# Causal masks of an attention kernel: added to the scores by matmuls with the identity, where GpSimd multiplied behind the exponentials

## The chip, the cores and the metric

The kernel runs on all 8 cores of one Trainium2 chip. The metric is the device time in microseconds of the slowest core. The program is the same on every core; core 2b + h works on batch row b and on the query blocks of parity h. Engines are named as in the profile: PE (TensorE matmul), PEld (its weight loads), DVE (VectorE), ACT (ScalarE), POOL (GpSimd), SP (the engine that issues most DMAs).

## The reference, cut to what matters

One transformer layer: attention, add, layernorm, quantized feed-forward network, add, layernorm.

```python
q = rms_norm((x @ Wq) by heads, q_g)          # 16 heads; only the first 32 of 64 columns are used
kv = x @ Wkv
k = rms_norm((kv @ Wk) by heads, k_g)         # 32 columns a head
v_c = (kv @ Wv) by heads                      # 32 columns a head
scores = jnp.einsum('bhtr,bhsr->bhts', q[..., :32], k) / sqrt(64)
scores = jnp.where(causal, -jnp.inf, scores)  # keys behind the query are masked out
probs = softmax(scores)
out_c = jnp.einsum('bhts,bhsd->bhtd', probs, v_c)
x = layernorm(x + out @ Wo)
# FFN: weights quantized to -1, 0, 1 by their mean; activations to 8 bits by their row's maximum
x = layernorm(x + bitlinear(silu(bitlinear(x, w_gate)) * bitlinear(x, w_up), w_down))
```

Batch 4, 4096 positions, width 1024, inner width 4096.

## The kernel before, in words

**Attention** (`attention()`, L801 on) goes over 4 tiles of 512 queries (`tc`), 4 groups of 4 heads (`gi`) and, for each, over blocks of 128 keys (`sc`). There are 8 key blocks for the first tile, 16, 24 and 32 for the others, thus 4 x (8 + 16 + 24 + 32) = 320 steps. In a step PE makes four score matmuls (L830), one a head, each with 32 rows of the array (`tile_position=(32 * j, 0)`), each into a PSUM bank of its own in `ps_sc`; the four share the array. Keys lie on the partitions of the score, queries along its free axis. ACT takes the exponential in two halves of two heads each (L843) and writes bf16 into one of three buffers `PT`. Two steps later (`LAG = 2`) PE adds the columns up (`den_mms`, L785, weights of ones) and multiplies by the values (`pv_mms`, L796), both with 32 columns of the array a head.

**The mask.** Of each tile's key blocks the last 8 touch the diagonal, which makes 4 x 4 x 8 = 128 diagonal steps; their score matmuls cover only the columns from `stc` on (512, 384, 256 or 128 of them, twice each). Blocks come in pairs, one of the core's own parity (even `sc`) and one of the other (odd `sc`). Of the 128 columns from `stc` on, the even block is triangular, and the odd block is to be kept whole on cores with h = 1 and dropped whole on cores with h = 0. POOL does that behind the exponentials, for the four heads at once: L851 multiplies by the triangle `tri`, L856 by the core's flag `hflag`. `den_mms` of the step waits for that product.

**What is woven in.** `attention()` yields once a step, and twice a step when the FFN has begun (`ffn_on`). At a yield the program puts other work into the queues of the engines in an order that is fixed when the program is built. In the early part, these are the projections of the later queries and keys (L528, L547, L569, L578 on PE) and the stream of FFN weights (`stream_step`): load, sum of absolute values (L366 on DVE, L370 on ACT), quantize (L382, L385 on DVE), store as fp8. When these are over, each yield brings in matmuls of the FFN: `RATE / 2` is added to a credit, and the FFN takes four matmuls of 512 columns at a time from it (L1001 for the up and gate projections, L1124 for the down projection). So a step has 7 FFN matmuls on average. Every engine takes its instructions strictly in this order. In this part the four score matmuls stand one behind the other; in the early part the sums of the step before last (`den_mms`) stand between the first two and the last two. Behind the attention the rest of the FFN runs by itself.

**Others on POOL.** POOL also issues the loads of x (`load_x`, L146), takes the variance to the power -0.5 for the layernorms (L695, L698), and multiplies and rounds in the quantization of the FFN's inner activations (L1073), which DVE (L1076) and a transposing DMA finish ahead of L1124.

Of the kernel before, what the change touches and what calls it, by code (L numbers as in the profile page):

```python
# [7 lines left out]
F32 = mybir.dt.float32  # L8
# [99 lines left out]
def build_nc():  # L108
# [20 lines left out]
    with es:  # L129
# [3 lines left out]
        def pe(fn, after=(), sig=False):  # L133
            return P.op("tensor", fn, after, cT if sig else None)
# [4 lines left out]
        def dve(fn, after=()):  # L139
            return P.op("vector", fn, after, cV)  # L140

        def pool(fn, after=()):
            return P.op("gpsimd", fn, after, cG)
# [4 lines left out]
        def xpose(out, in_, s, after=()):  # L148
# [3 lines left out]
        psb = lambda name, shape, dt: es.enter_context(nc.psum_tensor(name, shape, dt))  # L152


        tri = sb("tri", [128, 128], BF16)
        bd32 = sb("bd32", [128, 128], BF16)
        ones32 = sb("ones32", [128, 32], BF16)
        mhalf = sb("mhalf", [128, 1], F32)
        epsc = sb("epsc", [128, 1], F32)
# [1 line left out]
        hflag = sb("hflag_sb", [128, 1], F32)  # L161
        gq = sb("gq", [128, 1], F32)
        negM = sb("negM", [128, 1], F32)
        wabs = sb("wabs", [128, 48], F32)
        wsum = sb("wsum", [128, 3], F32)
        swb = sb("swb", [128, 3], F32)
        wscl = sb("wscl", [128, 3], F32)
# [39 lines left out]
        wv = rv(16640, 256).bitcast(BF16)  # L207
        onesf = rv(16896, 128)
        grow = rv(17024, 64)
        wq = rv(6144, 4096).bitcast(BF16)  # L210
        xt = [rv(10240 + 2048 * k, 2048).bitcast(BF16) for k in range(2)]
        xqT = [S[:, 1024 * k:1024 * k + 1024].bitcast(BF16) for k in range(2)]
# [36 lines left out]
        t_eps = pool(lambda e: e.memset(epsc[:], 1e-6))  # L249
        pool(lambda e: e.memset(onesf, 1.0))  # L250
        pool(lambda e: e.memset(ones32[:], 1.0))
        t = pool(lambda e: e.memset(tri[:], 1.0))
        pool(lambda e: e.affine_select(tri[:], tri[:], [[1, 128]], ALU.is_ge, 0.0,
                                       base=0, channel_multiplier=-1), [t])
        t = pool(lambda e: e.memset(bd32[:], 1.0))
        for j in range(4):
            t = pool(lambda e, j=j: e.affine_select(
                bd32[:, 32 * j:32 * j + 32], bd32[:, 32 * j:32 * j + 32], [[0, 32]],
# [7 lines left out]

        t = dve(lambda e: e.scalar_tensor_tensor(gq[:], gcol[:, 0:1], 0.125, gcol[:, 1:2],
                                                 ALU.mult, ALU.mult), [t_small])
        t = dve(lambda e: e.tensor_mul(grow[:, 0:32], grow[:, 0:32], grow[:, 32:64]), [t_small])
        t = dve(lambda e: e.tensor_reduce(negM[:], grow[:, 0:32], AX, ALU.max,  # L270
                                          apply_absolute_value=True), [t])
# [164 lines left out]
        def inv_rms(t_sq, inv, banks):  # L436

            b2 = banks.take()
            p2 = banks.bufs[b2]
            for n, (i, tt) in enumerate(t_sq):  # L440
                t2 = pe(lambda e, i=i, n=n, p2=p2: e.matmul(
                    p2, bd32[:], sq[i], start=(n == 0), stop=(n == len(t_sq) - 1)),
                    [tt, banks.free[b2], t_const], n == len(t_sq) - 1)
            for i, tt in t_sq:
                sq_free[i] = t2
            k = n_rs[0] % 2
            n_rs[0] += 1
            t3 = act(lambda e, k=k, p2=p2: e.activation(  # L448
                rsb[k], p2, AF.Ln, bias=epsc[:, 0:1], scale=inv), [t2, t_eps, rs_free[k]])
            banks.give(b2, t3)  # L450
            t4 = act(lambda e, k=k: e.activation(rsb[k], rsb[k], AF.Exp, scale=-0.5), [t3])
            return k, t4
# [360 lines left out]
        def attention():  # L813
# [3 lines left out]
            for tc in range(4):  # L817
                while t_tile[tc] is None:
                    next(proj_it, None)
                for gi in range(4):  # L820
                    smax = 8 * tc + 8
                    for sc in range(smax):
# [3 lines left out]
                        kc = ((2 * (j0 // 4) + sc % 2) * 4 + gi) * 512 + (j0 % 4) * 128  # L826
                        old = pend.pop(0) if len(pend) == LAG else None
                        t_sc = []
                        for j in range(4):
                            t = pe(lambda e, j=j, gi=gi, tc=tc, kc=kc, stc=stc: e.matmul(  # L830
                                ps_sc[:, j * 512 + stc:j * 512 + 512],
                                khat[32 * j:32 * j + 32, kc:kc + 128],
                                qn[32 * j:32 * j + 32, tc * 2048 + gi * 512 + stc:
                                   tc * 2048 + gi * 512 + 512],
                                start=True, stop=True, tile_position=(32 * j, 0)),
                                (sc_free[j // 2] if j % 2 == 0 else [])
                                + (t_tile[tc] if sc == gi == j == 0 else []), j % 2 == 1)
                            if j % 2 == 1:
                                t_sc.append(t)
                                if j == 1 and old and not ffn_on[0]:  # L840
                                    den_mms(*old[0])
                        for hf in range(2):
# [3 lines left out]
                                bias=negM[:, 0:1]),  # L846
                                [t_sc[hf], t_gq] + (pt_free[pp] if hf == 0 else []))
                            sc_free[hf] = [t]
                        if sc >= 8 * tc:
                            if sc % 2 == 0:  # L850
                                t = pool(lambda e, pp=pp, stc=stc: e.tensor_tensor(  # L851
                                    PTr[pp][:, :, stc:stc + 128], PTr[pp][:, :, stc:stc + 128],
                                    tri.rearrange("p (r n) -> p r n", r=1)
                                    .broadcast_to((128, 4, 128)), ALU.mult), [t, t_const])
                            else:
                                t = pool(lambda e, pp=pp, stc=stc: e.tensor_scalar(  # L856
                                    PTr[pp][:, :, stc:stc + 128], PTr[pp][:, :, stc:stc + 128],
                                    hflag[:, 0:1], None, ALU.mult), [t, t_small])
                        if ffn_on[0]:
                            yield 1  # L860
                            if old:
# [478 lines left out]
```

How the kernel before makes its waits and increments, by code:

```python
            def run(e):  # L62
                for fn, waits, inc in ops:
                    for h, v in waits:
                        e.wait_ge(h, v)
                    if fn is None:
                        continue
                    inst = fn(e)
                    if inc is not None:
                        inst.then_inc(inc[0], inc[1])
```

## Time and profile before

| | |
|---|---|
| median of 3 runs | 1576.91 us (1574.1 to 1585.49) |
| the profiled execution | 1579.0 us; span of its slowest core (core 4) 1577.5 us |
| spans of the 8 cores | 1565.3 to 1577.5 us |
| PE busy | 1312.7 us, 83% of the span |
| DVE, ACT, POOL busy | 805.3, 828.2, 327.6 us |
| chain that ended last | PE 60%, DVE 11%, DMA 10%, issue 8%, ACT 8%, POOL 1% |

PE's busy time is a union of pipelined matmuls. The chain is followed back from the last instruction; "issue" is time in it for which the profile shows no cause. The granted clock is the share of full speed that TensorE was given. In the trace of core 4 the first exponentials and masks are at 90 us, the first FFN matmuls at about 560 us, the end of attention at 1149 us. I call 88 to 560 us the early part, 560 to 1165 us the late part. Of the 16 groups of 8 diagonal steps nine lie in the early part (72 steps) and seven in the late part (56 steps).

### The profile page before, as it was taken

The numbers are of one execution on the slowest core, as the hardware profiler recorded it, in microseconds if no ns is written. First come the engines' busy times: TensorE is split into PE (matmuls) and PEld (weight loads), VectorE is DVE, ScalarE is ACT, GpSimd is POOL, SyncE is SP. The second block draws the span as 40 slices with busy tenths as digits, with TensorE's granted clock in tenths as the row PEclk, the third lists the DMA queues.
The fourth block names the chain that finished last, engine by engine and source line by source line (L and its number), as shares of the span: only waits on it lengthen the run. The fifth ranks groups of instructions, "written<-read, shape, count | busy, mean of one in ns | idle before, by whom it ended". The sixth has DMA issues, their size and how long they took to land.

```text
span 1577.5 us, 22882 instructions; the slowest of 8 cores (1565.3 to 1577.5 us)
## 1 busy us (share of the span) xinstructions
PE 1312.7 (83%) x7494; PEld 441.5 (28%) x7494; DVE 805.3 (51%) x1158; ACT 828.2 (53%) x998; POOL 327.6 (21%) x350
## 2 busy tenths in 40 slices
PE   2667578789976787879988998989985999999997
PEld 0212122222211122222322222222232444444443
DVE  2327864666555656642664234323364767273743
ACT  2576466687976765757766786847810121020200
POOL 1025421244210203050203212050113002020320
PEclk9966566755866589989999999989998999999999
DMA  9996795768545377663353633162336868586783
GB/s 251 305 282 182 228 260 160 195 206 267 187 154 187 99 245 221 216 134 107 128 147 117 157 105 91 60 161 61 130 125 183 270 201 220 187 202 227 178 222 119
DMA packets 146513, 283.06 MB, mean 179 GB/s; under 512 B 91744, under 2 KB 92000, under 8 KB 133088
## 3 DMA queue, kind: packets, MB, share of 16 engines
q1 hardware_dynamic: 144816, 272.70, 56.9%
q0 software_dynamic: 1584, 8.91, 3.5%
q8 instruction: 64, 1.05, 0.3%
q14 instruction: 49, 0.40, 0.1%
HBM read 235.96 MB, written 33.55 MB: 171 GB/s over the span
## 4 chain that ended last, share of the span: by engine, by line
PE 60%; DVE 11%; DMA 10%; issue 8%; ACT 8%; POOL 1%; SPq 1%; DVEq 0%; ACTq 0%; POOLq 0%
PE ps_w L1001 13%; PE ps_sc L1001 8%; PE ps_sc L830 7%; PE ps_w L1124 6%; ACT PT L843 5%; DMA R<-wffn 5%; PE ps_sc L1124 4%; PE ps_den L785 4%; PE ps_w L547 3%; PE ps_pv L796 3%; PE ps_w L716 2%; DVE qb L382 2%; PE ps_pv L1001 2%; PE ps_den L1001 2%; DMA khat<-wq 2%
## 5 line engine op out<-in xcount | busy, mean ns | idle before, releaser
L843 ACT ACTIVATE PT<-ps_sc,negM 128x1024 bf16<-128x1024 f32 (+3 forms) x640 | 593.7, 984 | 202.4 <-PE ps_sc L830 199.3
L1001 PE MATMUL ps_w<-R,S 128*128 128x512 fp8e4 x1032 | 272.1, 389 | 22.4 <-DVE xsC L957 6.7
L830 PE MATMUL ps_sc<-qn,khat 32*128 32x512 bf16 (+3 forms) x1280 | 210.9, 403 | 61.4 <-ACT PT L843 57.3
L851 POOL TENSOR_TENSOR PT<-PT,tri 128x512 bf16<-128x512 bf16 x64 | 80.7, 1262 | 418.7 <-ACT PT L843 417.2
L785 PE MATMUL ps_den<-PT,ones 128*32 128x512 bf16 (+3 forms) x1280 | 132.9, 405 | 8.1 <-DVE S L774 7.1
L1124 PE MATMUL ps_w<-R 128*128 128x512 fp8e4 x448 | 121.8, 402 | 20.9 <-DMA R<-R 18.4
L856 POOL TENSOR_SCALAR PT<-PT,hflag_sb 128x512 bf16<-128x512 bf16 x64 | 119.7, 1870 | 75.3 <-ACT PT L843 74.3
L796 PE MATMUL ps_pv<-PT,vtok 128*32 128x512 bf16 (+3 forms) x1280 | 130.6, 399 | 0.0
L1001 PEld LDWEIGHTS ps_w<-R,S 128*128 128x128 bf16 x1032 | 83.6, 99 | 164.8 <-issue 97.5
L830 PEld LDWEIGHTS ps_sc<-qn,khat 32*128 32x128 bf16 x1280 | 54.0, 93 | 262.3 <-issue 257.5
L1014 ACT ACTIVATE R<-ps_w,xsT 128x512 f32<-128x512 f32 x76 | 52.3, 688 | 131.9 <-PE ps_w L1001 121.0
L1020 DVE SCALAR_TENSOR_TENSOR R<-R,ps_w 128x512 f32<-128x512 f32 x76 | 52.0, 685 | 113.2 <-ACT R L1014 110.9
L695 POOL TENSOR_SCALAR mv<-mv 128x1 f32<-128x1 f32 x32 | 10.3, 322 | 449.1 <-DVE mv L694 434.6
L1073 POOL TENSOR_SCALAR R<-R,fs 128x512 f32<-128x512 f32 x96 | 66.9, 707 | 153.5 <-DVE fs L1065 115.1
L1076 DVE TENSOR_SCALAR R<-R 128x512 bf16<-128x512 f32 x128 | 59.8, 508 | 75.2 <-POOL R L1073 48.8
L1014 ACT ACTIVATE R<-ps_sc,xsT 128x512 f32<-128x512 f32 x34 | 23.4, 687 | 133.8 <-PE ps_sc L1001 100.7
L1001 PE MATMUL ps_sc<-wb,S 128*128 128x512 fp8e4 x352 | 78.3, 379 | 0.0
L547 PE MATMUL ps_w<-R 128*128 128x512 bf16 x192 | 73.1, 525 | 4.4 <-ACT S L448 2.7
L385 DVE TENSOR_SCALAR qb<-qb 128x2048 fp8e4<-128x2048 int8 x48 | 65.9, 1372 | 13.6 <-DVE qb L382 8.4
L1037 DVE TENSOR_REDUCE am<-R 128x1 f32<-128x512 f32 x96 | 65.9, 686 | 10.3 <-DVE R L1032 0.5
L1032 DVE TENSOR_TENSOR R<-R,ps_w 128x512 f32<-128x512 f32 x68 | 46.7, 686 | 47.1 <-PE ps_w L1001 45.6
L785 PEld LDWEIGHTS ps_den<-PT,ones 128*32 128x32 bf16 x1280 | 33.7, 95 | 121.4 <-issue 118.4
(199 smaller groups left out, 1507.8 us busy)
## 6 DMA issues: line engine op xcount, KB each, us to landing
R<-wffn SPq DMA_DIRECT2D x65, 1024.0 KB, 7.0
R<-scr_w SPq DMA_DIRECT2D x128, 512.0 KB, 4.5
wb<-scr_w SPq DMA_DIRECT2D x64, 512.0 KB, 5.1
scr_w<-qb SPq DMA_DIRECT2D x48, 256.0 KB, 6.1
khat<-wffn SPq DMA_DIRECT2D x11, 1024.0 KB, 12.2
vtok<-wffn SPq DMA_DIRECT2D x11, 1024.0 KB, 8.2
R<-xt POOLq DMA_DIRECT2D x7, 1024.0 KB, 14.7
R<-scr_x SPq DMA_DIRECT2D x12, 512.0 KB, 5.8
```

Of the source, the lines that this page charges most:

```text
L385: t2 = st["fi"] = dve(lambda e, o=o: e.tensor_scalar(fq[o], fi, 1.0, None, ALU.min, saturate=False), [t, t_fq[o]])
L547: t1 = pe(lambda e, c=c, cc=cc, p1=p1: e.matmul(p1, wq[:, c * D + cc:c * D + cc + 128], x[:, c * 512:(c + 1) * 512], start=(c == 0), stop= ...
L785: pe(lambda e, j=j: e.matmul(ps_den[32 * j:32 * j + 32, stc:512], ones32[:], PT[pp][:, j * 512 + stc:j * 512 + 512], start=(sc == 0), stop ...
L796: t = pe(lambda e, j=j, h=h: e.matmul(ps_pv[32 * j:32 * j + 32, stc:512], vtok[:, h:h + 32], PT[pp][:, j * 512 + stc:j * 512 + 512], start ...
L830: t = pe(lambda e, j=j, gi=gi, tc=tc, kc=kc, stc=stc: e.matmul(ps_sc[:, j * 512 + stc:j * 512 + 512], khat[32 * j:32 * j + 32, kc:kc + 128 ...
L843: t = act(lambda e, hf=hf, pp=pp, stc=stc: e.activation(PTr[pp][:, 2 * hf:2 * hf + 2, stc:512], PSr[:, 2 * hf:2 * hf + 2, stc:512], AF.Exp ...
L851: t = pool(lambda e, pp=pp, stc=stc: e.tensor_tensor(PTr[pp][:, :, stc:stc + 128], PTr[pp][:, :, stc:stc + 128], tri.rearrange("p (r n) -> ...
L856: t = pool(lambda e, pp=pp, stc=stc: e.tensor_scalar(PTr[pp][:, :, stc:stc + 128], PTr[pp][:, :, stc:stc + 128], hflag[:, 0:1], None, ALU. ...
L1001: t = pe(lambda e, c=c, b=b, kw=kk[w], i=i: e.matmul(wring.bufs[b], xqT[u % 2][:, i * 1024 + c * 128:i * 1024 + c * 128 + 128], wbuf[kw][: ...
L1014: tt = act(lambda e, k=k, b=b, ti=ti: e.activation(tg[k], wring.bufs[b], AF.Tanh, scale=xsT[:, ti:ti + 1]), [t, t_xs[u], tg_free[k]])
L1073: t1 = pool(lambda e, cs=cs, hh=hh: e.tensor_scalar(hm[hh], hs.h[i][:, cs:cs + 512], fs[:, p + 6 + i:p + 7 + i], MAGIC, ALU.mult, ALU.add) ...
L1124: t = pe(lambda e, c=c, ic=ic, b=b, kw=kw, i=i: e.matmul(wring.bufs[b], hs.hqT[i][:, ic * 128:ic * 128 + 128], wbuf[kw][:, c * 512:(c + 1) ...
```

## The change: masks as matmuls

Two constants take the place of `tri`: `mskT`, which holds -1e30 where the key comes after the query and 0 elsewhere, and `mskH`, which holds (h - 1) x 1e30 everywhere, with `ident`, the identity, beside them. In a diagonal step a matmul with the mask as weights (128 x 128) and the identity as the moving operand (128 columns) is accumulated onto each head's scores in PSUM, before the exponential: two behind the first two score matmuls, two behind the last two. ACT now waits for them. The products on POOL are gone. `bd32` and `wabs` move to another place in SBUF, and so make room.

```diff
-        tri = sb("tri", [128, 128], BF16)
-        bd32 = sb("bd32", [128, 128], BF16)
+        ident = sb("ident", [128, 128], BF16)
+        mskT = sb("mskT", [128, 128], BF16)
+        mskH = sb("mskH", [128, 128], BF16)
...
-        t = pool(lambda e: e.memset(tri[:], 1.0))
-        pool(lambda e: e.affine_select(tri[:], tri[:], [[1, 128]], ALU.is_ge, 0.0,
-                                       base=0, channel_multiplier=-1), [t])
-        t = pool(lambda e: e.memset(bd32[:], 1.0))
+        t = pool(lambda e: e.memset(mskT[:], -1e30))
+        pool(lambda e: e.affine_select(mskT[:], mskT[:], [[1, 128]], ALU.is_ge, 0.0,
+                                       base=-1, channel_multiplier=-1), [t])
+        t = pool(lambda e: e.memset(ident[:], 1.0))
+        t = pool(lambda e: e.affine_select(ident[:], ident[:], [[1, 128]], ALU.is_ge, 0.0,
+                                           base=0, channel_multiplier=-1), [t])
+        pool(lambda e: e.affine_select(ident[:], ident[:], [[-1, 128]], ALU.is_ge, 0.0,
+                                       base=0, channel_multiplier=1), [t])
+        t_mskH = pool(lambda e: e.memset(mskH[:], 1.0))
...
+        t = dve(lambda e: e.tensor_scalar(hneg, hflag[:], 1e30, -1e30, ALU.mult, ALU.add),
+                [t_small])
+        t_mskH = dve(lambda e: e.tensor_scalar(mskH[:], mskH[:], hneg, None, ALU.mult),
+                     [t, t_mskH])
...
+                        diag = sc >= 8 * tc
+                        msk = mskH if sc % 2 else mskT
                         for j in range(4):
-                            t = pe(lambda e, j=j, gi=gi, tc=tc, kc=kc, stc=stc: e.matmul(
+                            t = pe(lambda e, j=j, gi=gi, tc=tc, kc=kc, stc=stc, diag=diag: e.matmul(
...
-                                start=True, stop=True, tile_position=(32 * j, 0)),
+                                start=True, stop=not diag, tile_position=(32 * j, 0),
+                                skip_group_check=True),
                                 (sc_free[j // 2] if j % 2 == 0 else [])
-                                + (t_tile[tc] if sc == gi == j == 0 else []), j % 2 == 1)
+                                + (t_tile[tc] if sc == gi == j == 0 else []),
+                                j % 2 == 1 and not diag)
                             if j % 2 == 1:
+                                if diag:
+                                    for jj in (j - 1, j):
+                                        t = pe(lambda e, jj=jj, stc=stc, msk=msk: e.matmul(
+                                            ps_sc[:, jj * 512 + stc:jj * 512 + stc + 128],
+                                            msk[:], ident[:], start=False, stop=True,
+                                            skip_group_check=True), [t_const, t_mskH], jj == j)
                                 t_sc.append(t)
...
-                        if sc >= 8 * tc:
-                            if sc % 2 == 0:
-                                t = pool(lambda e, pp=pp, stc=stc: e.tensor_tensor(
-                                    PTr[pp][:, :, stc:stc + 128], PTr[pp][:, :, stc:stc + 128],
-                                    tri.rearrange("p (r n) -> p r n", r=1)
-                                    .broadcast_to((128, 4, 128)), ALU.mult), [t, t_const])
-                            else:
-                                t = pool(lambda e, pp=pp, stc=stc: e.tensor_scalar(
-                                    PTr[pp][:, :, stc:stc + 128], PTr[pp][:, :, stc:stc + 128],
-                                    hflag[:, 0:1], None, ALU.mult), [t, t_small])
```

On PE in the early part, two diagonal steps of the second query tile stood so before (L547 is a projection, L441 the sum of squares for a norm):

```order
L547 MATMUL ps_w<-R 128x512 x4
L830 MATMUL ps_sc<-qn,khat 128x512 x2
L785 MATMUL ps_den<-PT,ones 32x512 x4
L830 MATMUL ps_sc<-qn,khat 128x512 x2
L796 MATMUL ps_pv<-PT,vtok 32x512 x4
L441 MATMUL ps_w<-S,bd 128x512 x2
L830 MATMUL ps_sc<-qn,khat 128x512 x2
L785 MATMUL ps_den<-PT,ones 32x512 x4
L830 MATMUL ps_sc<-qn,khat 128x512 x2
L796 MATMUL ps_pv<-PT,vtok 32x512 x4
L547 MATMUL ps_w<-R 128x512 x4
```

The first of these two steps in the changed kernel, whose lines are numbered 15 to 17 higher:

```order
L562 MATMUL ps_w<-R 128x512 x4
L847 MATMUL ps_sc<-qn,khat 128x512 x2
L860 MATMUL ps_sc<-ident,mskT 128x128 x2
L800 MATMUL ps_den<-PT,ones 32x512 x4
L847 MATMUL ps_sc<-qn,khat 128x512 x2
L860 MATMUL ps_sc<-ident,mskT 128x128 x2
L811 MATMUL ps_pv<-PT,vtok 32x512 x4
L456 MATMUL ps_w<-S,R 128x512 x2
```

The order of everything else is as it was; two mask matmuls stand behind each pair of score matmuls.

On PE in the late part, two diagonal steps of the last group of heads stood so before:

```order
L830 MATMUL ps_sc<-qn,khat 128x384 x4
L1001 MATMUL ps_w<-R,S 128x512 x4
L785 MATMUL ps_den<-PT,ones 32x512 x4
L796 MATMUL ps_pv<-PT,vtok 32x512 x4
L1001 MATMUL ps_w<-R,S 128x512 x4
L830 MATMUL ps_sc<-qn,khat 128x384 x4
L1001 MATMUL ps_w<-R,S 128x512 x4
L785 MATMUL ps_den<-PT,ones 32x512 x4
L796 MATMUL ps_pv<-PT,vtok 32x512 x4
```

The same two steps in the changed kernel:

```order
L847 MATMUL ps_sc<-qn,khat 128x384 x2
L860 MATMUL ps_sc<-ident,mskT 128x128 x2
L847 MATMUL ps_sc<-qn,khat 128x384 x2
L860 MATMUL ps_sc<-ident,mskT 128x128 x2
L1016 MATMUL ps_w<-R,S 128x512 x4
L800 MATMUL ps_den<-PT,ones 32x512 x4
L811 MATMUL ps_pv<-PT,vtok 32x512 x4
L1016 MATMUL ps_w<-R,S 128x512 x4
L847 MATMUL ps_sc<-qn,khat 128x384 x2
L860 MATMUL ps_sc<-ident,mskH 128x128 x2
L847 MATMUL ps_sc<-qn,khat 128x384 x2
L860 MATMUL ps_sc<-ident,mskH 128x128 x2
```

The run of four score matmuls is now two pairs with full-array matmuls between them. The number of FFN matmuls between two steps is unchanged. Over the kernel PE has 4 x 128 = 512 matmuls and weight loads more, and POOL has 128 instructions fewer.

## Rows read from the trace of the kernel before

**Rows 1.** Span and mean granted clock of two of the eight cores.
```profile
core 4: 1577.5 us, clock 0.861
...
core 7: 1565.3 us, clock 0.872
```

**Rows 2.** Busy time by stretch, core 4; last columns are granted clock, DMA share, GB/s.
```profile
88.00:560.00 472.00, 360.86 (x1910) 95.98 (x1910) 274.35 (x298) 335.40 (x422) 129.12 (x92) 0.63 0.66 201
560.00:1165.00 605.00, 532.48 (x3716) 161.36 (x3713) 270.81 (x401) 406.79 (x448) 122.68 (x124) 0.95 0.45 135
1165.00:1578.00 413.00, 385.22 (x1761) 172.78 (x1759) 236.28 (x434) 47.42 (x69) 68.99 (x108) 0.98 0.70 200
```

**Rows 3.** Page, groups of instructions: form xcount | busy, mean ns | idle before, releaser.
```profile
L843 ACT ACTIVATE PT<-ps_sc,negM 128x1024 bf16<-128x1024 f32 (+3 forms) x640 | 593.7, 984 | 202.4 <-PE ps_sc L830 199.3
...
L851 POOL TENSOR_TENSOR PT<-PT,tri 128x512 bf16<-128x512 bf16 x64 | 80.7, 1262 | 418.7 <-ACT PT L843 417.2
...
L856 POOL TENSOR_SCALAR PT<-PT,hflag_sb 128x512 bf16<-128x512 bf16 x64 | 119.7, 1870 | 75.3 <-ACT PT L843 74.3
```

**Rows 4.** Chain of waits of the early part (88 to 560 us), by line.
```profile
by line: issue 13.0%; PE ps_sc L830 12.7%; PE ps_w L547 10.7%; ACT PT L843 7.8%; PE ps_den L785 5.8%; PE ps_w L716 5.5%; PE ps_pv L796 5.4%; DVE qb L382 3.8%; DVE S L778 3.6%; PE ps_w L528 3.5%; ACT R L370 3.2%; DMA scr_w<-qb 3.0%; DMA R<-w
```

**Rows 5.** All instructions of L856: min/median/max ns; last, who waited (us, times).
```profile
L856 POOL TENSOR_SCALAR PT<-PT,hflag_sb x64: 1562/1571/3347, 94.0 to 1147.0; 128x512 bf16<-128x512 bf16 x64
...
  PE ps_den L785: 0.9, 2
```

**Rows 6.** Chain of waits in order of time: first and last of the eight pieces of POOL products.
```profile
379.19 2.60 POOL PT L856
...
1146.99 1.57 POOL PT L856
```

**Rows 7.** Timeline of PE, late part: start, length, instruction.
```profile
1132.90 0.34 PE L830 MATMUL ps_sc<-qn,khat 32*128 32x384 bf16 x2 [0.58 <-ACT PT L843]
...
1134.68 1.04 PE L1001 MATMUL ps_w<-R,S 128*128 128x512 fp8e4 x4
...
1135.65 0.34 PE L830 MATMUL ps_sc<-qn,khat 32*128 32x384 bf16 x4
...
1138.41 0.29 PE L830 MATMUL ps_sc<-qn,khat 32*128 32x256 bf16 x4
...
1138.63 1.04 PE L1001 MATMUL ps_w<-R,S 128*128 128x512 fp8e4 x4
```

**Rows 8.** Timeline of PE behind the attention.
```profile
1239.93 3.62 PE L1001 MATMUL ps_sc<-R,S 128*128 128x512 fp8e4 x16
1243.38 1.89 PE L1001 MATMUL ps_den<-R,S 128*128 128x512 fp8e4 x8
```

**Rows 9.** Page, groups: weight loads of the full array.
```profile
L1001 PEld LDWEIGHTS ps_w<-R,S 128*128 128x128 bf16 x1032 | 83.6, 99 | 164.8 <-issue 97.5
```

**Rows 10.** Timeline of PE in the early part.
```profile
177.01 0.39 PE L830 MATMUL ps_sc<-qn,khat 32*128 32x256 bf16 x2
177.33 0.51 PE L785 MATMUL ps_den<-PT,ones 128*32 128x384 bf16 x4
177.77 0.40 PE L830 MATMUL ps_sc<-qn,khat 32*128 32x256 bf16 x2
```

**Rows 11.** Busy time (columns as in rows 2) of two groups of diagonal steps.
```profile
845.00:870.00 25.00, 18.40 (x148) 5.71 (x144) 10.45 (x20) 13.87 (x19) 16.49 (x16) 0.86 0.30 77
938.00:961.00 23.00, 22.24 (x172) 7.19 (x170) 7.56 (x11) 16.40 (x23) 10.85 (x8) 1.00 0.27 94
```

**Rows 12.** Timeline of DVE in an early group of diagonal steps.
```profile
379.12 1.23 DVE L385 TENSOR_SCALAR qb<-qb 128x2048 fp8e4<-128x2048 int8 x1 [0.17 <-DVE qb L382]
...
383.04 1.91 DVE L385 TENSOR_SCALAR qb<-qb 128x2048 fp8e4<-128x2048 int8 x1 [0.17 <-DVE qb L382]
```

**Rows 13.** Early part of core 7, columns as in rows 2.
```profile
88.00:560.00 472.00, 355.21 (x1990) 97.91 (x1986) 279.75 (x304) 347.20 (x435) 128.80 (x92) 0.69 0.69 207
```

**Rows 14.** Waits of ACT in the late part (us in total, times, longest).
```profile
ACT PT L843 <- PE ps_sc L830: 156.1, 109, 8.4
```

More of the change, by code:

```diff
@@ L163, in build_nc @@
         negM = sb("negM", [128, 1], F32)
-        wabs = sb("wabs", [128, 48], F32)
         wsum = sb("wsum", [128, 3], F32)
@@ L209, in build_nc @@
         grow = rv(17024, 64)
+        bd32 = rv(17088, 64).bitcast(BF16)
+        wabs = rv(17152, 48)
+        hneg = rv(17200, 1)
         wq = rv(6144, 4096).bitcast(BF16)
@@ L251, in build_nc @@
         pool(lambda e: e.memset(ones32[:], 1.0))
-        t = pool(lambda e: e.memset(tri[:], 1.0))
-        pool(lambda e: e.affine_select(tri[:], tri[:], [[1, 128]], ALU.is_ge, 0.0,
-                                       base=0, channel_multiplier=-1), [t])
-        t = pool(lambda e: e.memset(bd32[:], 1.0))
+        t = pool(lambda e: e.memset(mskT[:], -1e30))
[7 more added lines that the diff above has]
+        t_mskH = pool(lambda e: e.memset(mskH[:], 1.0))
+        t = pool(lambda e: e.memset(bd32, 1.0))
         for j in range(4):
@@ L441, in inv_rms @@
                 t2 = pe(lambda e, i=i, n=n, p2=p2: e.matmul(
-                    p2, bd32[:], sq[i], start=(n == 0), stop=(n == len(t_sq) - 1)),
+                    p2, bd32, sq[i], start=(n == 0), stop=(n == len(t_sq) - 1)),
                     [tt, banks.free[b2], t_const], n == len(t_sq) - 1)
```

## The prediction, on record before the run

> **What bounds the kernel now.** I read the cores first. Their spans lie within 12 us of one another, and the core with the highest mean clock has the shortest span [rows 1]. Then the busy time by stretch [rows 2]. In the early part PE is busy for 361 of 472 us at a granted clock of 0.63, that is about a quarter of the time at the higher of its two levels (2.4 GHz) and the rest at the lower (1.2 GHz). In the late part it is busy for 532 of 605 us at 0.95, and behind the attention for 385 of 413 us. So from 560 us on the kernel is as long as PE's work, with little room; whatever is put on PE there comes off the end almost whole. In the early part the chain of waits goes through PE for nearly half of its length (the six PE lines shown make 43.6%), "issue" has 13.0%, and the rest is ACT, DVE and the stores and loads of the weight stream [rows 4]. There an added piece of PE work counts about half.
>
> The removed products come next. They take 80.7 + 119.7 = 200 us of POOL [rows 3], which is much, but off the path: POOL sat idle before L851 for 419 us, and PE waited for L856 0.9 us in two places [rows 5]. The reader is to see that the sums of a step come two steps after its exponentials, and that a product of 1.57 us fits in between. In the chain of waits the products have eight pieces, 7.66 us in all, one of 2.60 us early and seven with 5.06 us late; the largest and the one at the very end of attention are shown [rows 6].
>
> **The change, part by part.**
>
> *Late part, 56 diagonal steps.* The durations are PE's start-to-start times. Sixteen matmuls of 512 columns take 3.45 us [rows 8], so a column costs 0.42 ns and the 128 columns of a mask 0.054 us. A full-array matmul has weights to load, 0.099 us on average [rows 9]. When PE goes over between the score form (32 rows of the array) and the full array, it loses time: four FFN matmuls should take 4 x 0.2156 = 0.86 us, but the scores behind them start after 0.97; and scores of 256 columns, four at once, should take 0.11 us, but the FFN matmul behind them starts after 0.22 [rows 7]. Either way a switch costs 0.11 us.
> A diagonal step now goes scores, masks, scores, masks, FFN. The last switch is there already (the scores were followed by an FFN matmul, and a mask has the same full form), so two are new: 0.22 us. No row shows two full-array matmuls of 128 columns in a row. The second can start at once (0.054 us later, columns alone) or after its whole weight load (0.10 us). I take 0.10, since there is less streaming than loading; a pair then has 0.10 + 0.054 = 0.154 us, two pairs 0.31. Last, the four score matmuls shared the array and now run as two pairs, so one width is paid again: the mean width is 320 columns, 0.135 us. But some steps were split before, when the second pair waited for ACT, 0.58 us in the row shown [rows 7]; in the last group 3 of 8 were. So 0.08. Sum: 0.22 + 0.31 + 0.08 = 0.61 us a step, 34 us for 56.
> The bounds: columns alone, 0.22 us a step and 12 us in all; and every mask with a load of its own (0.61), three switches (0.33) and the sharing lost wholly (0.135), 1.07 us and 60 us.
> Some is hidden by waits that PE has anyway. In one group of eight diagonal steps PE is busy 22.2 of 23 us, in another 18.4 of 25 [rows 11]; about three of the seven groups look like the second, where PE waits for activations of the down projection. I let half of their 4.9 us vanish there, 7 us, and 2 us more in the waits for ACT. If this cover were gone it would all be paid. 34 - 9 = 25 us.
>
> *Early part, 72 diagonal steps.* The switch is the same at the lower level: 256 columns at twice 0.42 ns are 0.21 us, and the sums behind the scores start after 0.32 [rows 10]. A mask's columns take 0.107 us there, which covers the weight load. The sums stood between the pairs before, so no sharing is lost, and two switches are new: 4 x 0.107 + 0.22 = 0.65 us, or 0.53 us at the higher level; with a quarter at the higher, 0.62. Over 72 steps: 45 us. Half of it on the path: 22 us. The bounds are the columns alone, a quarter exposed (0.43 x 72 / 4 = 8 us), and loads, three switches and lost sharing, three quarters exposed (some 1.28 x 72 x 3/4 = 69 us).
>
> *The products removed.* Their pieces of the chain go, with a little of the "issue" around them: 3 us early, 7 us late. What is late next is the exponential itself, whose masked form now comes out one product earlier. Nothing hides behind the products on POOL's queue but the layernorm powers, L1073 and the loads of x, and those gain with them. DVE gains too: a quantizing instruction took 1.91 us while a product ran, and 1.23 us otherwise [rows 12], and a product took up to 3.35 us where the median is 1.57 [rows 5]. With 36 flag products early that is at most 36 x 0.68 = 24 us of DVE; by the share of its quantizing and reciprocal lines in the chain, 7.4% [rows 4], 2 us. The Trainium skill (GPSIMD Engine Reference, Specifications) says that POOL's SBUF interfaces are shared with VectorE, with contention for some DVE forms; by that rule, the trace agrees, and the sum stays as the rows make it.
>
> *At the start* POOL sets up three constants in place of one and DVE has two small instructions more. The first masks are needed at 90 us and PE is still waiting for x until well behind them: nothing.
>
> **Sum:** late 25 - 7 = 18, early 22 - 3 - 2 = 17, together 35 us. On the profiled execution of 1579.0 us that is 1614 us. That execution lies 2.1 us over the median of the runs shown, so I forecast **1612 us**.
>
> A rule against the change: the Trainium skill (TensorEngine Tiling (Array Packing), Key Properties) says that changing the tiling mode drains the TensorE. Its page TensorE: Matmul & The Clock Gate (Single matmul latency) gives a lone matmul a constant of 398 cycles of 2.4 GHz beside its columns, an estimate of 0.17 us for a drain. The rows show a loss at every such change, but 0.11 us. By the page's figure two switches would cost 0.11 us more a step, and the total would be about 9 us higher.
>
> **The rivals.**
>
> *Hidden (0.25).* PE has 73 us of idle time late and 111 us early [rows 2], and the masks might fall mostly into it, with weight loads that overlap (the 12 us bound less half, and 8 us early) and the products' 12 us back. That gives +2 to +15, about 1583 us. For it: ACT waits for scores and PE for ACT in turn. Against it: the late group that is busy 22.2 of 23 us.
>
> *The clock pays (0.12), faster.* The place is the early part, where PE runs at the lower level most of the time. Core 7 was granted 0.69 there [rows 13] against core 4's 0.63 and ended 12.2 us sooner, so 0.01 of early clock is worth about 2 us. Masks are full-array work in the gaps. If they lift the early clock by 0.15 (-30 us), the masks cost their columns alone (12 + 8 us) and the products give 8 us back, the kernel comes out near 1559 us. It decides from an early clock of about 0.75 on; below that the masks' price wins. The Trainium skill (TensorE: Matmul & The Clock Gate, Part 1) says that the throttled state is the default and activity releases it. By that rule, the trace agrees as far as the clock is 0.95 where PE is busy 88% and 0.63 where it is busy 76% [rows 2]. Against it: 288 masks of 0.107 us add some 9% to PE's early work at most, and core 7 has that clock with slightly less busy time.
>
> *The path through the exponentials (0.15), slower still.* The mask now stands between scores and exponential, and ACT already waits 156 us for scores in the late part [rows 14]. If each half of each exponential comes 0.3 us later where ACT or PE's own order has no slack, in half of the 128 steps, that adds 64 x 2 x 0.3 = 38 us to the part now counted as hidden; I take 30 of it: 1642 us.
>
> The forecast itself has 0.48.
>
> **Numbers.** About 1% (16 us) is what can be told from no change: 1561 to 1593. Slower by over 1%: forecast and the third rival, 0.63. Within 1%: 0.25. Faster: 0.12. The range reaches from 1562, which leaves out most of the clock case, to 1650, which holds the third rival; both upper bounds of the masks' price together would give 1687 and get the remaining tenth.
>
> **What would show it.** In the changed profile the steps are right if: the mask matmuls (512) start 0.10 us apart within a pair in the late part; scores and masks are 0.11 us apart beyond their columns; eight late diagonal steps take some 4 us longer in a group that is busy throughout, like the one at 938 us; the FFN behind the attention takes as long as before; the early clock stays within 0.03 of 0.63; POOL falls to some 130 us busy; DVE's L385 stays near 1.23 us. Wrong, if the early part ends no later than before, if the attention's end moves by less than 15 us, or if the early clock goes above 0.7.

## The result and the profile after

The changed kernel takes 1603.74 us (median of 4 runs, 1602.3 to 1605.38), the kernel before 1581.2 us in the same comparison (4 runs, 1574.1 to 1586.79). The ratio is 1.0143, with a 95% interval of 1.0103 to 1.0183: slower by 1.4%, some 22 us. The forecast was 35 us slower, 1612 us. Some executions of any of these kernels fall into a second, slower state, with a lower clock on one half of the cores; all times and ratios here are of executions outside it.

The page of the changed kernel (slowest core, core 7), its engines and groups; the columns are those of [rows 3]:

```profile
PE 1366.0 (85%) x8006; PEld 472.7 (29%) x8006; DVE 790.9 (49%) x1160; ACT 833.8 (52%) x998; POOL 129.8 (8%) x226
...
L868 ACT ACTIVATE PT<-ps_sc,negM 128x1024 bf16<-128x1024 f32 (+3 forms) x640 | 598.6, 986 | 223.8 <-PE ps_sc L847 116.7
```

POOL fell from 327.6 to 129.8 us, PE rose from 1312.7 to 1366.0 us, and ACT waits 21 us more in front of its exponentials than in [rows 3]. Half of the new line's instructions, those with the triangle (the flag's 256 have the same three times), with their shortest, middle and longest time in ns; below, who waited for the line:

```profile
L860 PE MATMUL ps_sc<-ident,mskT x256: 219/229/314, 93.6 to 1168.2; 128*128 128x128 bf16 x128
...
  ACT PT L868: 104.5, 92
```

The busy times by stretch of core 7, columns as in [rows 2]:

```profile
88.00:560.00 472.00, 376.63 (x2145) 109.22 (x2145) 256.35 (x286) 333.25 (x420) 10.61 (x20) 0.66 0.64 199
560.00:1185.00 625.00, 562.41 (x3971) 176.41 (x3970) 271.76 (x408) 417.05 (x455) 42.51 (x68) 0.95 0.45 133
```

The late part is still filled by PE. The early part does fewer DVE and ACT instructions in the same 472 us than [rows 2] and [rows 13]: it is behind. The chain of waits of this early part, by line, is to be held against [rows 4]; the masks (L860) hold 5.9% of it:

```profile
by line: issue 12.1%; PE ps_sc L847 12.0%; PE ps_w L562 8.2%; ACT PT L868 7.2%; DMA scr_w<-qb 6.1%; PE ps_sc L860 5.9%; PE ps_den L800 5.6%; PE ps_w L731 5.6%; PE ps_pv L811 5.3%; DVE S L793 4.3%; PE ps_w L543 3.9%; DVE qb L397 3.3%; ACT R 
```

The cores' spans lie 11 to 21 us apart in a run, so I use two landmarks, each the mean over the 8 cores of a profiled run: the start of the first FFN matmul (end of the early part) and the start of the last score matmul (end of the late part, but for a few us). They are in the answers on single lines. For core 4, first before, then after, the FFN line and the score line:

```profile
L1001 PE MATMUL ps_w<-R,S x1032: 376/379/634, 558.0 to 1497.0; 128*128 128x512 fp8e4 x172
...
L830 PE MATMUL ps_sc<-qn,khat x1280: 211/384/605, 88.6 to 1145.7; 32*128 32x512 bf16 x130, 32*128 32x256 bf16 x19, 32*128 32x384 bf16 x17, 32*128 32x128 bf16 x17
```
```profile
L1016 PE MATMUL ps_w<-R,S x1032: 376/379/634, 562.7 to 1507.0; 128*128 128x512 fp8e4 x172
...
L847 PE MATMUL ps_sc<-qn,khat x1280: 211/384/605, 90.2 to 1156.2; 32*128 32x512 bf16 x130, 32*128 32x256 bf16 x19, 32*128 32x384 bf16 x17, 32*128 32x128 bf16 x17
```

Here are the landmarks of all kernels that ran, with the ratio of their runs to the kernel before. The clock is the mean granted clock of the eight cores from 88 to 540 us. The landmarks and the clock come from one execution of each kernel. The fifth column does not: it is the mean span of the eight cores over all runs of the kernel, less that of the runs of the kernel before, with a 95% interval of 1 to 3 us to either side. It is steadier than the ratio, which follows the slowest core alone. For the change, the runs of before are those beside e1 to e8.

| kernel | early part ends | late part lasts | early clock | mean core, over before | ratio (95% interval) |
|---|---|---|---|---|---|
| before | 553.4 | 587.1 | 0.65 | 0 | 1 |
| the change | 565.9 | 595.4 | 0.68 | +21 | 1.0143 (1.0103 to 1.0183) |
| e1 no mask, no product | 552.3 | 575.9 | 0.64 | -12.5 | 0.9922 (0.9891 to 0.9952) |
| e2 masks and products | 562.6 | 602.6 | 0.69 | +24.4 | 1.0157 (1.0123 to 1.0191) |
| e3 masks late only | 554.2 | 594.6 | 0.65 | +9.4 | 1.0052 (1.0032 to 1.0072) |
| e4 masks early only | 562.7 | 584.4 | 0.68 | +9.0 | 1.0053 (1.0033 to 1.0074) |
| e5 masks twice | 571.4 | 605.2 | 0.72 | +37.3 | 1.0248 (1.0218 to 1.0279) |
| e6 one column | 559.0 | 590.0 | 0.65 | +10.1 | 1.0112 (1.0077 to 1.0147) |
| e7 masks last (late) | 564.3 | 587.1 | 0.68 | +12.0 | 1.0062 (1.0033 to 1.0091) |
| e8 mix | 555.4 | 581.3 | 0.65 | -2.2 | 1.0000 (0.9980 to 1.0020) |
| e9 late flags | 556.1 | 584.1 | 0.65 | 0.0 | 1.0001 (0.9987 to 1.0014) |
| e10 flags, triangle on POOL | 553.9 | 583.0 | 0.66 | -1.3 | 0.9983 (0.9956 to 1.0010) |

What follows the late part takes 430 to 433 us in all of them. Kernels with the same masks in the early part (before, e3; the change, e2, e4, e7) differ by up to 3.3 us there, with the same late part (before, e4) by 2.7; I read nothing smaller from one landmark.

**PE's order in time.** A diagonal step of the late part on core 7 and the end of attention, timeline of PE (start, length, instruction):

```profile
1155.47 0.34 PE L847 MATMUL ps_sc<-qn,khat 32*128 32x384 bf16 x2
1155.74 0.28 PE L860 MATMUL ps_sc<-ident,mskT 128*128 128x128 bf16 x2
1155.96 0.34 PE L847 MATMUL ps_sc<-qn,khat 32*128 32x384 bf16 x2
1156.22 0.28 PE L860 MATMUL ps_sc<-ident,mskT 128*128 128x128 bf16 x2
1156.35 1.03 PE L1016 MATMUL ps_w<-R,S 128*128 128x512 fp8e4 x4
...
1173.53 0.23 PE L800 MATMUL ps_den<-PT,ones 128*32 128x128 bf16 x4
1173.59 0.23 PE L811 MATMUL ps_pv<-PT,vtok 128*32 128x128 bf16 x4
```

Scores to masks is 0.27 us: 384 columns (0.16) and 0.11 for the switch. Masks to scores is 0.22: two times 0.054 and 0.11. The last masks to the FFN matmul is 0.13: two times 0.054, and no switch. From the first score to the FFN it is 0.88 us, where [rows 7] has 0.22 for 256 columns, so 0.27 for 384. The step costs 0.61 us more. The last two rows belong to the end of attention, where [rows 6] had a product on the path and PE now waits for none.

An early step of the same core, in a stretch at the lower level of the clock (12 us around it have a granted clock of 0.51):

```profile
378.37 0.61 PE L847 MATMUL ps_sc<-qn,khat 32*128 32x512 bf16 x2
378.91 0.39 PE L860 MATMUL ps_sc<-ident,mskT 128*128 128x128 bf16 x2
379.23 0.62 PE L800 MATMUL ps_den<-PT,ones 128*32 128x512 bf16 x4
```

A pair of masks with its new switch takes 0.32 us, so the two pairs of a step take the 0.65 us that the forecast has for this level.

### The profile page after: what moved, and what is told of

Its sections match the earlier page's. It is cut to its first block, busy times and chain, and to the rows that moved or that the text cites. A ratio compares the mean times of both kernels' runs of the same rounds, so it can differ in the third digit from the quotient of the medians.

```text
span 1603.7 us, 23530 instructions; the slowest of 8 cores (1587.4 to 1603.7 us)
## 1 busy us (share of the span) xinstructions
PE 1366.0 (85%) x8006; PEld 472.7 (29%) x8006; DVE 790.9 (49%) x1160; ACT 833.8 (52%) x998; POOL 129.8 (8%) x226
## 4 chain that ended last, share of the span: by engine, by line
PE 63%; DVE 11%; DMA 9%; issue 7%; ACT 7%; SPq 1%; POOL 1%; DVEq 0%; ACTq 0%; POOLq 0%
PE ps_w L1016 14%; PE ps_sc L1016 7%; PE ps_sc L847 7%; PE ps_w L1139 6%; ACT PT L868 4%; PE ps_den L800 4%; PE ps_sc L1139 4%; DMA R<-wffn 4%; PE ps_pv L811 3%; PE ps_sc L860 3%; PE ps_w L562 2%; DVE S L793 2%; PE ps_w L731 2%; DVE qb L397 2%; PE ps_pv L1016 2%
## 5 line engine op out<-in xcount | busy, mean ns | idle before, releaser
L847 PE MATMUL ps_sc<-qn,khat 32*128 32x512 bf16 (+3 forms) x1280 | 220.3, 398 | 50.6 <-ACT PT L868 46.7
L1088 POOL TENSOR_SCALAR R<-R,fs 128x512 f32<-128x512 f32 x96 | 67.1, 709 | 420.1 <-DVE fs L1080 358.4
L400 DVE TENSOR_SCALAR qb<-qb 128x2048 fp8e4<-128x2048 int8 x48 | 58.9, 1227 | 18.8 <-DMA scr_w<-qb 11.5
L1150 DVE SCALAR_TENSOR_TENSOR R<-ps_w,fs,R 128x512 f32<-128x512 f32 x16 | 12.0, 751 | 112.3 <-PE ps_w L1139 86.1
L562 PE MATMUL ps_w<-R 128*128 128x512 bf16 x192 | 63.2, 466 | 4.6 <-ACT S L463 2.3
L447 ACT ACTIVATE S<-ps_w 128x512 bf16<-128x512 f32 x48 | 28.8, 600 | 60.2 <-PE ps_w L584 30.2
(207 smaller groups left out, 1581.2 us busy)
```

The lines of the kernel that those rows point to most:

```text
L400: t2 = st["fi"] = dve(lambda e, o=o: e.tensor_scalar(fq[o], fi, 1.0, None, ALU.min, saturate=False), [t, t_fq[o]])
L562: t1 = pe(lambda e, c=c, cc=cc, p1=p1: e.matmul(p1, wq[:, c * D + cc:c * D + cc + 128], x[:, c * 512:(c + 1) * 512], start=(c == 0), stop= ...
L847: t = pe(lambda e, j=j, gi=gi, tc=tc, kc=kc, stc=stc, diag=diag: e.matmul(ps_sc[:, j * 512 + stc:j * 512 + 512], khat[32 * j:32 * j + 32, ...
L1088: t1 = pool(lambda e, cs=cs, hh=hh: e.tensor_scalar(hm[hh], hs.h[i][:, cs:cs + 512], fs[:, p + 6 + i:p + 7 + i], MAGIC, ALU.mult, ALU.add) ...
```

## The experiments

**e1: neither masks nor products.** It prices the removal alone.

```diff
-                        diag = sc >= 8 * tc
+                        diag = False
```

> No masking at all: neither the mask matmuls nor the products on POOL (the output leaves causality out in the diagonal blocks). It prices the removal of POOL's products alone. Theory A (the products were nearly off the path, the chain of waits held 7.7 us of them): 6 to 12 us faster than before. Theory B (the removal relieves DVE and the down projection's queue on POOL by much more, and the masks' price of 50 us or more is paid in full and hidden behind that relief): 25 us or more faster than before. The early clock stays within 0.02 of before by A; if the masks themselves raised it in the changed kernel, it is not raised here.

Measured: 0.9922, 12 us faster; the late part is 11.2 us shorter, the early part ends 1 us sooner, the early clock is that of before. Theory A holds at the upper end of its 6 to 12 us, B falls. The relief lies in the late part alone, and mostly in two places: from the narrowed scores (384 columns) of one late group to those of the next it is 4.5 us in the period that starts at 677 us and 5.2 us in the one at 1038 us (times of core 4 before, lengths as means over all eight cores; the five other periods are within 1.2 us). Both periods hold a down projection; the third that holds one, from 851 us, gives 1.0. In the chain of waits before (core 4), at the second place, one reads why:

```profile
1038.51 1.46 POOL PT L856
...
1040.07 0.11 POOL PT L851
1040.17 1.02 issue
1041.19 0.70 POOL R L1073
...
1042.06 0.55 DVE R L1076
...
1043.29 3.04 DMA R<-R
```

The quantizing product L1073, which the down projection's transposed activations wait for, stands behind two mask products in POOL's order. In e1 (core 3), where this product is L1088, POOL goes straight on, one pair each 1.8 us when nothing else is waited for:

```profile
1030.16 1.39 POOL L1088 TENSOR_SCALAR R<-R,fs 128x512 f32<-128x512 f32 x2 [3.50 <-DVE R L1091]
1032.00 1.39 POOL L1088 TENSOR_SCALAR R<-R,fs 128x512 f32<-128x512 f32 x2 [0.45 <-DVE R L1091]
```

**e2: masks on PE, products kept on POOL.**

```diff
+                        if sc >= 8 * tc:      # the products of before, unchanged
+                            if sc % 2 == 0:
+                                t = pool(lambda e, pp=pp, stc=stc: e.tensor_tensor(
...
```

> Mask matmuls on PE as in the change and the products on POOL kept behind the exponentials (the product changes nothing any more). The flag mask is here identity weights with a moving column that is repeated, the same sizes. Theory A: 6 to 12 us over the changed kernel, so 29 to 35 us over before. Theory B: 25 us or more over the changed kernel. In the late groups of diagonal steps that meet a down projection (four of seven), theory A has the same lengths as in the changed kernel within 1 us; B has them 2 us or more longer each.

Measured: 1.0157, which is 1.4 parts in a thousand or 2 us over the change, and 4 us by the mean core. That is under the 6 to 12 expected (the interval of the ratios alone would still allow 6), and theory B is out. By the landmarks the late part is 7.2 us longer than in the change and the early part 3.3 us shorter, which is within its scatter. So with masks on PE the products' removal gives back 7 us late, less than the 11 without masks. The price of masks is 15.5 us late where the products stay (602.6 - 587.1) and 19.5 us where they are gone (595.4 - 575.9). The two differ by 4 us, hardly more than the scatter. As I read them, the two terms of my sum are not independent: a wait for the down projection's activations hides part of the masks, and when the wait goes, so does the cover. No run tests this by itself.

**e3 and e4: masks in one part only,** products in the other.

```diff
-                        diag = sc >= 8 * tc
+                        diag = sc >= 8 * tc and ffn_on[0]          # e3; e4 has: and not ffn_on[0]
+                        # products on POOL in the other part, as before
```

> Masks by matmul in the late part only (56 steps), products on POOL in the early part as before. By the landmarks of the two traces the late part grew by 9 us: 1.5 to 3 us in each of three groups that PE fills, about nothing in the four with down projections. Theory A: 7 to 11 us over before. Rival (the late growth came from what the early part handed over, another clock or another order of the waits): less than 4 us.

> Masks by matmul in the early part only (72 steps), products on POOL in the late part as before. By the landmarks the first FFN matmul came 12 us later (mean over the cores). Theory A: 9 to 15 us over before, with the early clock 0.02 to 0.03 higher than before, since the masks fill PE's gaps. Rival (the early part hides the masks and only scatters): within 4 us of before.

Measured: 1.0052 (8 us) and 1.0053 (8 us). Late part of e3 7.5 us longer, as expected. Early part of e4 ends 9.3 us later at a clock of 0.68; in time it is just under the 9 to 15 expected, the clock as expected. The two sum to 16.6 us; the change has 22.6 with an interval of 16 to 29, so they may be all of it. By the mean core they sum to 18.4 of 21 us.

**e5: each mask twice.**

```diff
-                                    for jj in (j - 1, j):
+                                    for jj in (j - 1, j, j - 1, j):
```

> Each mask matmul issued twice (eight a step; the scores of masked keys get -2e30 in place of -1e30). Theory A (a late mask costs its 128 columns, 0.054 us, and the rest of the step's price is in the switches of the array's form; about 0.6 of it reaches the end, and a third of the early columns): 4 x 0.054 x 56 x 0.6 = 7 us late and 4 x 0.107 x 72 / 3 = 10 us early, so 12 to 20 us over the changed kernel. Theory C (each mask pays a weight load of 0.10 us of its own): 35 us or more over it. If the early clock rises further (0.69 or more), the early part gives some back.

Measured: 1.0248, 16.6 us over the change by the ratios, inside the 12 to 20 of theory A; theory C is out. Late 9.8 us, early 5.5 us more, and the early clock went up again, to 0.72. The timeline (core 5) has four masks in the place of two, 0.33 us to the next scores where two take 0.22, so each costs its columns:

```profile
1170.26 0.40 PE L860 MATMUL ps_sc<-ident,mskT 128*128 128x128 bf16 x4
1170.59 0.34 PE L847 MATMUL ps_sc<-qn,khat 32*128 32x384 bf16 x2
```

**e6: the same matmuls with one moving column** (127 of 128 query columns stay unmasked).

```diff
-                                            ps_sc[:, jj * 512 + stc:jj * 512 + stc + 128],
-                                            msk[:], ident[:], start=False, stop=True,
+                                            ps_sc[:, jj * 512 + stc:jj * 512 + stc + 1],
+                                            msk[:], ident[:, 0:1], start=False, stop=True,
```

> The same number of mask matmuls and switches, but one moving column in place of 128 (127 of 128 query columns stay unmasked). It leaves the switches, the weight loads and the lost sharing, and takes the columns away. Theory A: 7 us late and up to 10 us early less than the changed kernel, so 8 to 16 us under it. Theory C: no change within 4 us, since the weight load would hold each matmul.

Measured: 1.0112, 5 us under the change by the ratios; by the landmarks 5.4 us late and 6.9 us early, 12 together. The ratio lies between the theories, and its interval (1.0077 to 1.0147) contains both; the slowest cores of these four runs stood further out than elsewhere. The mean core is 11 us under the change, and with the landmarks that agrees with theory A. The timeline (core 3) speaks against a weight load for each: two masks and a switch in 0.14 us.

```profile
1135.66 0.20 PE L860 MATMUL ps_sc<-ident,mskT 128*128 128x1 bf16 x2
1135.80 0.39 PE L847 MATMUL ps_sc<-qn,khat 32*128 32x512 bf16 x2
```

With one column the early clock is that of before (0.65), with the columns 0.68.

**e7: late, the four masks behind the four scores.**

```diff
-                                if diag:
-                                    for jj in (j - 1, j):
+                                if diag and (j == 3 or not ffn_on[0]):
+                                    for jj in range(4) if ffn_on[0] else (j - 1, j):
```

> In the late part the four scores stand one behind the other again and the four masks behind them, with the first half of the exponential signalled after the second mask. Takes two switches (0.22 us) and the lost sharing (0.08 to 0.16 us) out of a late step. Theory A: 0.3 to 0.38 us x 56 x 0.6 = 10 to 13 us under the changed kernel. Rival (the first exponential now waits for the last two scores, which wait for ACT, and that costs as much as the switches): within 4 us of the changed kernel or above it.

Measured: 1.0062, some 13 us under the change, 9 us by the mean core; late part 8.3 us shorter. That is theory A or just under it, and not the rival. The step (core 3) is 0.50 us for the 0.88 of the change, from the first score to the FFN matmul:

```profile
1142.44 0.34 PE L847 MATMUL ps_sc<-qn,khat 32*128 32x384 bf16 x4
1142.71 0.40 PE L860 MATMUL ps_sc<-ident,mskH 128*128 128x128 bf16 x4
1142.94 1.03 PE L1019 MATMUL ps_w<-R,S 128*128 128x512 fp8e4 x4
```

**e8: early as before, late four together, the flag masks in the scores' own form.** A constant mask needs no identity: 32 rows that hold (h - 1) x 3e28 against ones.

```diff
+                            if j == 3 and diag and sc % 2:
+                                for jj in range(4):
+                                    t = pe(lambda e, jj=jj, stc=stc: e.matmul(
+                                        ps_sc[:, jj * 512 + stc:jj * 512 + stc + 128],
+                                        mskH[32 * jj:32 * jj + 32, :],
+                                        ones32[32 * jj:32 * jj + 32, 0:1].broadcast_to((32, 128)),
+                                        start=False, stop=True, tile_position=(32 * jj, 0),
...
```

> What the runs point to as best: products on POOL in the early part as before, masks by matmul in the late part, four together behind the four scores, and the constant (flag) masks in the scores' own form (32 rows of weights, four heads at once), so without a switch. Theory A: PE pays 0.05 us in an odd step and 0.22 us in an even one, 56 x 0.14 x 0.6 = 5 us, and gets the late relief of 11 us seen without any mask: 3 to 9 us faster than before. Rival (the relief is only to be had where PE is not loaded more, or the exponential waits): within 3 us of before or slower.

Measured: 1.0000 (0.9980 to 1.0020), not the 3 to 9 us expected. That is within the 3 us of its rival. By the landmarks of the profiled execution the late part is 5.8 us shorter than before and the mean span over the cores is 1566.5 against 1572.1 us, but most of that is the scatter of one execution: over all runs the mean core gains 2.2 us (0.3 to 4.1), and the slowest core nothing that can be told. The mechanism is seen in the timeline (core 3): four flag masks add 0.06 us to a step, 0.33 us from score to FFN for 384 columns.

```profile
1121.87 0.34 PE L851 MATMUL ps_sc<-qn,khat 32*128 32x384 bf16 x4
1122.05 0.22 PE L863 MATMUL ps_sc<-ones,mskH 32*128 32x128 bf16 x4
1122.20 1.04 PE L1045 MATMUL ps_w<-R,S 128*128 128x512 fp8e4 x4
```

**e9: late flag masks only; e10: flag masks in both parts,** the triangle on POOL, early part of e9 as before.

```diff
-                        diag = sc >= 8 * tc
+                        diag = sc >= 8 * tc and ffn_on[0] and sc % 2 == 1    # e9; e10 without ffn_on
```

> Only the flag masks of the late part (28 steps) are matmuls, in the scores' own form (no switch, 0.054 us a step, under 2 us in all) behind all four scores; the triangle and the whole early part stay on POOL. Theory A (the late relief of 11 us is POOL's queue ahead of the down projection's activations, mostly the longer flag products): late part 4 to 9 us shorter than before, total 2 to 8 us faster. Rival (the triangle products keep the down projection waiting just as long, so the relief is lost): late part within 2 us of before, total the same.

> The flag masks are matmuls in the scores' own form in both parts, two behind each pair of scores; the triangle stays on POOL. Late, this keeps the lost sharing (0.08 to 0.16 us in 28 steps) but has no switch. Early, a flag step pays 2 x 0.107 us of columns and no switch, 36 x 0.21 = 8 us raw, a third of it at the end. Theory A: early 1 to 4 us later than before, late 2 to 7 us shorter, total within 4 us of before; the early clock not over 0.01 higher. If the clock answers to masks in this form too, it is 0.67 or more.

Measured: 1.0001 (0.9987 to 1.0014) and 0.9983 (0.9956 to 1.0010). The late parts are 3.0 and 4.1 us shorter, each in one execution and at the edge of what the landmarks can tell; by the mean core the kernels are at 0.0 and -1.3 us. The late part of e9 lies between its theories, its total is the rival's; e10 is as its theory A has it. The triangle's products still stand in front of L1073 (L1098 in e9, core 4), and POOL waits 4.57 us for an exponential before it can do one:

```profile
1044.42 1.15 POOL L876 TENSOR_TENSOR PT<-PT,tri 128x512 bf16<-128x512 bf16 x1 [4.57 <-ACT PT L868]
1045.55 1.36 POOL L1098 TENSOR_SCALAR R<-R,fs 128x512 f32<-128x512 f32 x2
```

The shares fit: in the two periods where e1 found 4.5 and 5.2 us, e9 finds 2.1 and 1.2, and e8, without any late product, 4.4 and 3.3. The early clock of e10 is 0.66, 0.01 over before. No version is faster than the kernel before, in time of the slowest core, by more than can be told; e1 shows that all masking there is worth 12 us.

## Why the prediction came out right, and where its sizes were off

The sign and the mechanism were right: masks on PE lengthen both parts, and the relief from POOL's products is smaller. The size was 22 us and not 35. That 1603.74 lies only 8 us from 1612 is in part luck: the runs of the kernel before have a median 4 us higher here than the three that the forecast started from.

- **What bounds each part:** right. Late masks show in the end through PE, and the tail is unchanged. In the group that is busy throughout, at 944 us on core 4, the eight steps were to cost some 4 us more, and the period is 4.3 us longer.
- **The price of a late step,** 0.61 us: the sum is what the trace shows for 384 columns, but made up otherwise. The switches are 0.11 us each, as read from [rows 7]. The second mask of a pair comes 0.054 us after the first, not 0.10: the weight load is hidden (e5, e6), so the two pairs take 0.22 and not 0.31. The sharing lost is more than the 0.08 taken, in every step that ran together before; in the last group of core 4 only two of the eight steps were split, not three. That the two errors cancel in the 0.61 is luck.
- **Late masks, 34 us raw and 25 on the path:** too high. 19.5 us were found with the products gone, so 14 us hide and not 9. The periods without a down projection pay: 1.2, 3.5 and 4.3 us over before in those that start at 596, 751 and 944 us (core 4 before; means over eight cores). In the three that hold one, the change is 2.5 us under, 0.1 over and 1.7 under before; the two below it are those where e1 found the relief.
- **Late relief, 7 us:** 11.2 us alone (e1), 7.2 us with masks (e2). The chain of waits named the place, the products in front of L1073. PE waits there for the down projection's activations and not for a product, so [rows 5] alone would have missed it. Late together I forecast +18, and +8.3 came.
- **Early part, 22 - 5 = +17:** +12.5 in the change, +9.3 in e2 and e4. The relief of 5 is not there (e1: 1 us). DVE's L385 did fall to 1.23 us, 65.9 to 58.9 us in all, but the waits have no instruction that waited for it. (The 1.23 us of [rows 12] was not a time without a product, either: it began 0.07 us before the product of [rows 6], and there the product took 2.60 us.) The raw price of a step, 0.65 us, is what the timeline shows. What reaches the end is too high: the change, e4 and e7 have the same early part, and by their mean it ends 11 us after that of before and 12 us after that of e1, and not 22. Two terms too large with opposite signs, 22 and 5, brought 17 close to 12.5, which is luck.
- **The clock, a term that the sum left out.** The early clock rose by 0.03 with the masks and by 0.04 more with twice as many; it did not rise with one-column masks. This is the clock rival's mechanism at a fifth of the strength that it needed. No run held the clock still, so what it gave back is an estimate, made in two ways. Taken within the profiled runs, cores with a higher early clock end their early part sooner, by 2.1 us for 0.01 (one slope through the 96 cores of the twelve kernels, with much scatter, and with no such slope in e1 and e4); 0.03 is then worth 6 us. And e6, with the switches but hardly any columns, ends its early part 6.7 us after e1 at nearly the same clock, 0.4 of the 16 us that the switches add up to. The columns, 31 us, should then cost 13 us; the change, e4 and e7 lie only 5.3 us over e6, and the second set of e5 costs 7.1 us more. That leaves 6 to 8 us, the same. If this is right, 0.4 of the masks' work was on the path early, not far from the half that was forecast, and the rise of the clock gave about a third of that back.
- **The rival through the exponentials** is there as a wait, 104.5 us in which ACT waits for masks, but its 30 us did not come. Late, e7 delays the first exponential further and is faster. Early, no run separates this path from PE's own length; ACT's idle time before the exponentials grew by 16 us there (7 us late, means over the cores), and e10, whose flag masks also stand before the exponentials, ends its early part only 0.5 us later.
- **The rule on drains:** every row shows 0.11 us for a switch, and the forecast without the higher price was closer. The 0.17 us for a drain was an estimate from the constant in the Trainium skill (TensorE: Matmul & The Clock Gate, Single matmul latency), and no run shows it.

The step that was mis-sized most is what of the masks' work reaches the end. I took 25 of 34 late and 22 of 45 early; 19.5 and about 11 to 12 did. (One sum of the prediction is off as well: its two upper bounds with its 12 us of relief make 1577 + 60 + 69 - 12 = 1694 us and not 1687, and nothing else rests on it.)

## What to carry to other kernels

Work put on the engine that fills the span costs its full length only in the stretches where that engine never waits (4.3 of some 4.9 us in the late group at 944 us); count those stretches one by one. When small matmuls of another array form are woven in, the switch (0.11 us here) is dearer than 128 columns (0.054 us), so put them together, or in the form of their neighbours: e7 and e8 took a step's price from 0.61 to 0.23 and 0.06 us. And an off-path engine can hold the path by its order: look at what is queued behind the instruction, not only at who waits for it.

## What the runs showed of the hardware that was not expected

Two full-array matmuls of 128 columns in a row start 0.054 us apart although their weight loads last 0.098 us each (four in a row as well, e5), and with one column two of them take some 0.03 to 0.06 us (e6). TensorE's mean granted clock from 88 to 540 us, a part that it spends mostly at the lower of its two levels, was 0.65 before and with one-column masks (e6), 0.68 with the masks, 0.72 with each mask twice (e5), and 0.66 with flag masks in the 32-row form (e10). In the four kernels with the same early masks (the change, e2, e4, e7) it is 0.68 or 0.69, and in the five without any there (before, e1, e3, e8, e9) it is 0.64 or 0.65.
